# Attention with two-sided maxima: ScalarE presets the score banks, the row product goes, and the up projection moves ahead of the second maxima product

## The reference

```python
h = _layernorm(x, axis=-1) * (1 + ca) + sa
x = x + ga * _L0_attn_ref(h, ...)
h = _layernorm(x, axis=-1) * (1 + cb) + sb
x = x + gb * _L0_ffn_ref(h, ...)
```

## Time and profile before

| what | us |
|---|---|
| median of three runs | 906.31 |
| the profiled execution | 895.69 |
| its span | 893.96 |
| TensorE busy | 813.2 |
| VectorE busy | 637.1 |
| GpSimd busy | 662.7 |
| ScalarE busy | 397.2 |

### The profile page before, as it was taken

How to read it: one execution, slowest core, us unless ns; L and a number is a source line. 1 busy time by engine, 2 the same in 40 slices (tenths; PEclk the granted TensorE clock), 3 DMA queues, 4 the chain that set the end, 5 groups by cost and what they waited for, 6 DMA issues and landing times.

```text
span 894.0 us, 14690 instructions
## 1 busy us (share of the span) xinstructions
PE 813.2 (91%) x5118; PEld 485.9 (54%) x5118; DVE 637.1 (71%) x1156; ACT 397.2 (44%) x650; POOL 662.7 (74%) x348
## 2 busy tenths in 40 slices
PE   4689999999999999999999999999999977968581
PEld 2445555555555555555555555555555444368581
DVE  8987777777777777777777777777776757646022
ACT  3654444444444444444444444444444433336340
POOL 2579998898987878787878787878777856632333
PEclk8979999999999999999999999999999999969796
DMA  9101001010101011111011111101010000078683
GB/s 246 31 1 14 13 14 25 14 25 13 25 13 26 13 26 14 27 20 26 6 26 25 22 25 14 24 14 14 13 13 15 12 13 1 19 238 269 213 314 89
DMA packets 84330, 43.91 MB, mean 49 GB/s; under 512 B 57632, under 2 KB 73376, under 8 KB 84192
## 3 DMA queue, kind: packets, MB, share of 16 engines
q1 hardware_dynamic: 83232, 40.86, 18.2%
q0 software_dynamic: 1024, 2.10, 0.7%
HBM read 36.51 MB, written 6.16 MB: 48 GB/s over the span
## 4 chain that ended last, share of the span: by engine, by line
PE 82%; DVE 8%; DMA 4%; POOL 2%; issue 2%; ACT 1%; POOLq 0%; SPq 0%; DVEq 0%
PE ps_o L456 25%; PE ps_m L422 9%; PE ps_x L410 8%; PE ps_s L440 7%; PE ps_s L442 6%; PE ps_s L446 6%; PE ps_s L444 6%; PE ps_s L473 3%; DMA moe<-xs_dram 3%; PE ps_s L464 3%; PE ps_s L595 2%; PE ps_s L586 2%; POOL xs_dram L953 2%; DVE mx L1097 1%; PE ps_s L377 1%
## 5 line engine op out<-in xcount | busy, mean ns | idle before, releaser
L939 POOL TENSOR_TENSOR acc<-acc,probs 128x1024 f32<-128x1024 f32 (+1 forms) x192 | 459.9, 2395 | 74.7 <-ACT probs L697 52.5
L1097 DVE TENSOR_REDUCE mx<-ps_m 128x2 f32<-128x1024 f32 x240 | 293.7, 1224 | 90.9 <-PE ps_m L422 90.3
L697 ACT ACTIVATE probs<-ps_s 128x1024 f32<-128x1024 f32 x256 | 248.8, 1024 | 157.7 <-PE ps_s L446 157.6
L456 PE MATMUL ps_o<-probs,c_all 128*64 128x512 f32 x1024 | 249.5, 608 | 0.0
L440 PE MATMUL ps_s<-q_hi,k_hi 64*128 64x512 f32 x512 | 102.6, 397 | 12.0 <-DVE x_sb L1153 12.0
L456 PEld LDWEIGHTS ps_o<-probs,c_all 128*64 128x64 f32 x1024 | 62.4, 136 | 93.2 <-issue 44.5
L422 PE MATMUL ps_m<-k_hi,q_hi 64*128 64x512 f32 x480 | 107.7, 444 | 4.0 <-DVE mx L1097 4.0
L939 POOL TENSOR_TENSOR acc<-probs 128x1024 f32<-128x1024 f32 (+1 forms) x32 | 75.4, 2357 | 48.3 <-ACT probs L697 47.8
L442 PE MATMUL ps_s<-q_hi,k_lo 64*128 64x512 f32 x512 | 101.4, 391 | 0.0
L446 PE MATMUL ps_s<-neg_row,one_row 64*128 64x512 f32 x512 | 101.3, 391 | 0.0
L444 PE MATMUL ps_s<-q_lo,k_hi 64*128 64x512 f32 x512 | 100.8, 389 | 0.0
(11 more groups left out here) (299 smaller groups left out, 1025.5 us busy)
## 6 DMA issues: line engine op xcount, KB each, us to landing
probs<-in_experts SPq DMA_DIRECT2D x15, 578.0 KB, 6.0
rr<-rd_dram SPq DMA_DIRECT2D x62, 128.0 KB, 3.1
wu<-in_wqk SPq DMA_DIRECT2D x16, 256.0 KB, 3.4
neg_row<-nm SPq DMA_DIRECT2D x256, 0.5 KB, 2.0
w_first<-in_experts SPq DMA_DIRECT2D x5, 578.0 KB, 5.2
rot<-in_experts SPq DMA_DIRECT2D x5, 578.0 KB, 5.0
hT<-in_experts SPq DMA_DIRECT2D x5, 578.0 KB, 5.6
xs_dram<-zero SPq DMA_DIRECT2D x2, 960.0 KB, 9.4
```

Of the source, the lines that this page charges most:

```text
L456: ins = nc.tensor.matmul(ps_o[64 * h:64 * h + 64, :], c_all[:, (p // HP) * TB + kt, :], probs[:, st % 4, h, :], start=(kt == 0), stop=(kt ...
L697: nc.scalar.activation(probs[:, st % 4, :, :], ps_s[:, 2 * (st % 2):2 * (st % 2) + 2, :], ACT.Exp, scale=SCALE).then_inc(s["probs"], 1)
L939: V.tensor_tensor(acc[:, half, heads, :], first, probs[:, st % 4, heads, :], ALU.add).then_inc(s["added"], 1)
L1097: V.reduce_max(mx[:, :, kh, qt], max_banks(q, n), AX.X).then_inc(s["max_reduced"], 1)
```

## The change

ScalarE writes minus the maximum into a step's two score banks before TensorE adds the three remaining products to them (`start=False`). For that the maxima are spread over all partitions: each of the 8 columns of `nm` goes to a row in DRAM, and two DMAs spread it to `neg_wide`. The copy's halves for the banks 2 and 3 wait for the denominators' copy and for the output's addition, in ScalarE's order. On TensorE `up` stands ahead of the group's second maxima product, and the second value product of a group behind denominators and outputs. On VectorE the order in a group is reduce, turn, reduce, lower, and lower is that of the same group's unit. `upper` follows the exponentials and one preset of its own group.

```diff
@@ tensor: score
-                ge(pe, s["probs"], n_step(p, st) - 2)
-                if kt == 0:
-                    pe.wait_ge(row_placed[half], 128 * (p + 1))
-                if kt == 1:
-                    ge(pe, s["den_read"], n_part(p, half) - 2)
-                    ge(pe, s["out_added"], n_part(p, half) - 3)
+                pe.wait_ge(s["preset"], n_step(p, st))
...
-                    nc.tensor.matmul(bank[h], k_hi[rows(h), p % 3, kc], q_hi[rows(h), p % 3, qc], start=True, stop=False)
+                    nc.tensor.matmul(bank[h], k_hi[rows(h), p % 3, kc], q_hi[rows(h), p % 3, qc], start=False, stop=False, skip_group_check=True)
...
-                for h in range(2):
-                    ins = nc.tensor.matmul(bank[h], one_row[rows(h), :], neg_row[rows(h), p % 2, qc], start=False, stop=True)
@@ tensor: outputs
-                                           g_all[:, p // HP, p % HP, :], start=True, stop=True)
+                                           g_all[:, p // HP, p % HP, :], start=(n == 0), stop=(n == 3))
@@ tensor: a group
                     score(p, 2 * g)
                     score(p, 2 * g + 1)
+                    if p + 2 <= LAST:
+                        up(p + 2, g)
                     if p < LAST:
                         maxima(p + 1, 2 * g + 1)
...
-                    if p + 2 <= LAST:
-                        up(p + 2, g)
-                    for n in (2 * g - 2, 2 * g - 1):
+                    def value_step(n):
                         if n >= 0:
                             pv(p, n)
                         elif p > 0:
                             pv(p - 1, NSTEP + n)
+
+                    value_step(2 * g - 2)
                     if g in (3, 7):
                         pe.wait_ge(s["probs"], n_step(p, 2 * g + 1))
...
+                    value_step(2 * g - 1)
@@ scalar
+            def preset(p, st):
+
+                half, kt = divmod(st, TB)
+                if p == 0 and st < 2:
+                    act.wait_ge(s["max_reduced"], NMAX - 1 + st)
+                ge(act, s["probs"], n_step(p, st) - 2)
+                if kt == 0:
+                    act.wait_ge(row_wide[half], 32 * (p + 1))
+                if kt == 1 and (p or half):
+                    ge(act, s["den_read"], n_part(p, half) - 2)
+                    nc.scalar.copy(ps_s[:, 2, :], neg_wide[:, half, 0, :])
+                    ge(act, s["out_added"], n_part(p, half) - 3)
+                    nc.scalar.copy(ps_s[:, 3, :], neg_wide[:, half, 1, :]).then_inc(s["preset"], 1)
+                else:
+                    nc.scalar.copy(ps_s[:, 2 * (st % 2):2 * (st % 2) + 2, :], neg_wide[:, half, :, :]).then_inc(s["preset"], 1)
...
+            preset(0, 0)
+            preset(0, 1)
             for p in range(NPAIR):
                 for g in range(NGRP):
                     if g == 0 and p > 0:
                         den_out(p - 1, 0, ps_s[:, 2, :])
+                        preset(p, 1)
                     if g == 4 and p > 0:
                         den_out(p - 1, 1, ps_s[:, 2, :])
+                    if g == 4:
+                        preset(p, 9)
...
-                    if g == 0 and 2 <= p + 1 <= LAST:
-                        upper(p + 1, NGRP - 1)
-                    if g > 0 and p + 2 <= LAST:
-                        upper(p + 2, g - 1)
                     expo(p, 2 * g)
                     expo(p, 2 * g + 1)
+                    if g < NGRP - 1:
+                        preset(p, 2 * g + 2)
+                    elif p < LAST:
+                        preset(p + 1, 0)
+                    if p + 2 <= LAST:
+                        upper(p + 2, g)
+                    if g not in (3, NGRP - 1):
+                        preset(p, 2 * g + 3)
@@ vector
                     if p < LAST:
                         reduce_max(p + 1, 2 * g)
-                    q, u = (p + 2, g - 1) if g else (p + 1, NGRP - 1)
-                    if 2 <= q <= LAST:
-                        lower(q, u)
+                    if p + 2 <= LAST:
+                        turn(p + 2, g)
                     if p < LAST:
                         reduce_max(p + 1, 2 * g + 1)
                         if g % 4 == 3:
                             neg_max(p + 1, g // 4)
                     if p + 2 <= LAST:
-                        turn(p + 2, g)
+                        lower(p + 2, g)
@@ sync
                 for h in range(2):
                     for n in range(4):
-                        row = neg_row[64 * h:64 * h + 1, q % 2, half * HALF + n * P:half * HALF + (n + 1) * P]
-                        sp.dma_start(row.bitcast(F32), nm[:, half, h, n:n + 1].bitcast(F32)).then_inc(row_placed[half], 16)
+                        sp.dma_start(mr_dram[half, h:h + 1, n * P:(n + 1) * P], nm[:, half, h, n:n + 1]).then_inc(row_out[half], 16)
+
+            def max_spread(q, half):
+
+                sp.wait_ge(row_out[half], 128 * (q + 1))
+                if q:
+                    sp.wait_ge(s["preset"], n_step(q - 1, TB * half + TB - 1))
+                for h in range(2):
+                    sp.dma_start(neg_wide[:, half, h, :],
+                                 mr_dram[half, h:h + 1, :].to_broadcast([P, HALF])).then_inc(row_wide[half], 16)
...
                 if p > 0:
-                    if p < LAST + 1:
-                        max_rows(p, 1)
+                    max_rows(p, 1)
                     den_cols(p - 1, 0)
                     inv_rows(p - 1, 0)
+                    max_spread(p, 1)
                     inv_spread(p - 1, 0)
                 if p < LAST:
                     max_rows(p + 1, 0)
                 if p > 0:
                     den_cols(p - 1, 1)
                     inv_rows(p - 1, 1)
+                if p < LAST:
+                    max_spread(p + 1, 0)
+                if p > 0:
                     inv_spread(p - 1, 1)
```

More of the change, by code:

```diff
@@ L91, in build @@
         hi_of, lo_of = (q_hi, k_hi), (q_lo, k_lo)
-        one_row = sb("one_row", [P, P], F32R)
-        neg_row = sb("neg_row", [P, 2, S], F32R)
+        neg_wide = sb("neg_wide", [P, 2, 2, HALF])
         probs = sb("probs", [P, 4, 2, HALF])
@@ L96, in build @@
         mx = sb("mx", [P, 2, 2, TB])
-        nm = sb("nm", [P, 2, 2, 4], F32R)
+        nm = sb("nm", [P, 2, 2, 4])
         den = sb("den", [P, HALF])
@@ L107, in build @@
         rt_sb = sb("rt_sb", [P, 12, TB * E])
+        mr_dram = nc.dram_tensor("mr_dram", [2, 2, HALF], F32, kind="Internal").ap()
         rd_dram = nc.dram_tensor("rd_dram", [2, 2, HALF], F32, kind="Internal").ap()
@@ L211, in build @@
             "max_row": "both heads' maxima of half the queries, negated (vector)",
-            "scores": "both heads' scores of a step, less the maximum (tensor)",
+            "preset": "a step's score banks hold minus the maximum (scalar)",
+            "scores": "both heads' scores of a step, added to it (tensor)",
             "probs": "their probabilities (scalar)",
@@ L250, in build @@
         up_in = sem("up_in")
-        row_placed = [sem(f"row_placed{n}") for n in range(2)]
+        row_out = [sem(f"row_out{n}") for n in range(2)]
+        row_wide = [sem(f"row_wide{n}") for n in range(2)]
         den_cols_in, inv_out, inv_in = sem("den_cols_in"), sem("inv_out"), sem("inv_in")
@@ L439, in score @@
                 for h in range(2):
-                    nc.tensor.matmul(bank[h], k_hi[rows(h), p % 3, kc], q_hi[rows(h), p % 3, qc], start=True, stop=False)
+                    nc.tensor.matmul(bank[h], k_hi[rows(h), p % 3, kc], q_hi[rows(h), p % 3, qc], start=False, stop=False, skip_group_check=True)
                 for h in range(2):
-                    nc.tensor.matmul(bank[h], k_lo[rows(h), p % 3, kc], q_hi[rows(h), p % 3, qc], start=False, stop=False)
+                    nc.tensor.matmul(bank[h], k_lo[rows(h), p % 3, kc], q_hi[rows(h), p % 3, qc], start=False, stop=False, skip_group_check=True)
                 for h in range(2):
-                    nc.tensor.matmul(bank[h], k_hi[rows(h), p % 3, kc], q_lo[rows(h), p % 3, qc], start=False, stop=False)
-                for h in range(2):
-                    ins = nc.tensor.matmul(bank[h], one_row[rows(h), :], neg_row[rows(h), p % 2, qc], start=False, stop=True)
+                    ins = nc.tensor.matmul(bank[h], k_hi[rows(h), p % 3, kc], q_lo[rows(h), p % 3, qc], start=False, stop=True, skip_group_check=True)
                 ins.then_inc(s["scores"], 1)
@@ L1004, in then @@
                 dve.wait_ge(s["vector_step"], seq[0])
[L1006 to L1010, removed]
+            V.memset(ones[:], 1.0).then_inc(s["constants"], 1)
             def statistics(src, tiles):
@@ L1100, in neg_max @@
                 dve.wait_ge(s["max_reduced"], NMAX * q + TB * (half + 1))
-                ge(dve, row_placed[half], 128 * q)
+                ge(dve, row_out[half], 128 * q)
                 V.tensor_reduce(nm[:, half, :, :], mx[:, :, :, 4 * half:4 * half + 4].rearrange("p h k t -> p h t k"),
@@ L1378, in max_rows @@
```

(12 more changed lines are left out.)

## The result

The changed kernel takes 1078.31 us in the median of four runs (1068.44 to 1081.58), the kernel before, beside it, 903.71 (899.53 to 908.09): a ratio of 1.191, with an interval of 1.181 to 1.202. It is slower, as forecast, but by 175 us and not by 32. The time lies far outside the range of 892 to 955. Its profiled span is 1074.9.

What follows compares the result with a forecast made beforehand. The prediction took TensorE to bound the kernel before and a chain through VectorE the plain groups after. Halves of 3 x 5.07 + 8.22 = 23.43 against 22.07 gave +35, together with the ends +32: 938 us, range 892 to 955.

Steps and rivals of the forecast that it cites:

- The row DMAs keep their count and size: On SP's queue, the DMAs moving the maxima: said to stay the same in count and size, with no cost given.
- Four DMAs of broadcast per pair: The max_spread DMAs on SP's queue behind inv_rows: hidden, since SP waited some 2 us for inv_out there anyway.
- the start: At the kernel's beginning, two presets ahead of the first exponential: +1 us.
- Rival 3: Denominators' columns land late, so the reciprocal pushes turn by 0.5 us per half: +13, 951 us; chance 0.12.
- pair 14: Pair without up projection, so without the chain: its 8 groups could give 3.7 us back, 3 taken.
- The chain of the plain group: First maxima product, scores, up, turn, second reduction, next maxima product: 5.07 us a group, where it was 5.03.
- The division: In groups 2 and 6, VectorE's division catches GpSimd's addition 0.3 us after its start, running from 5.2 to 7.81.
- Rival 1: The division issues before GpSimd's addition and costs 0.68 us: total change -10.5, 896 us; chance 0.28.
- The closing group: Group 3 or 7, with denominators and output product: 6.56 plus 1.66 from the late division, 8.22 us instead of 6.98.
- Presets: ScalarE's 16 copies of 128x1024 into PSUM per pair: 1.02 us each, low end 0.92, hidden under the group.
- Rival 4: ScalarE becomes the bound, only from a preset of 1.45 us on; at 1.6, near 970 us; chance 0.04.
- Rival 2: TensorE stays the bound because a row of the chain overlaps: -47 us, with the ends 857; chance 0.04.

Runs made afterwards that it cites:

- e2: The changed kernel, with the row DMAs writing to SBUF as before and two 2 KB DMAs per half carrying the rows to DRAM: 950.17 us, ratio 1.058.
- e1: The changed kernel with SP's queue reordered, denominators' columns ahead of the row DMAs and inv_rows and inv_spread ahead of max_spread: 958.3 us, ratio 1.066.
- e3: The kernel before, with only its maxima rows sent through DRAM in 4-byte pieces and brought back by two 2 KB DMAs: 1034.92 us, ratio 1.153.
- e7: The kernel before plus eight DMAs of nm per half behind the columns, 4-byte pieces side by side in an unread DRAM buffer: 1053.78 us, one run.
- e8: e7 with the 4-byte pieces 256 bytes apart in DRAM: 901.08 us, one run.
- e4: The kernel before with only the new order on TensorE, VectorE and ScalarE, the row product kept: 970.94 us, ratio 1.079.
- e5: e2 with its presets but the kernel before's order on TensorE and VectorE, both presets ahead of upper: 885.63 us, ratio 0.986 to the kernel before.
- e9: e5 with one step of the values' product moved ahead of the second maxima product: 952.46 us, ratio 1.052 to the kernel before.
- e6: e2 with the division moved behind the closing group's first reduction: 909.03 us, ratio 1.011 to the kernel before.

## Why the prediction was wrong, point by point

**The step that failed** is the sentence "The row DMAs keep their count and size", with nothing costed behind it: a term of the sum put at nothing. Count and size are kept; the destination isn't. It went from SBUF to pieces side by side in DRAM. The profile before had no row of such a DMA (the nearest, of the reciprocals, has pieces of 16 bytes, and would have said 1.7 us). By the text's own manner its cost should have been bounded from both sides. What the runs show in its place: the columns behind these DMAs land late (after 9.26 us in the half shown), VectorE stands 3.9 us for them in the mean and 114.1 in all, and a half takes 28.3 instead of the forecast 23.4. The neighbouring "Four DMAs of broadcast per pair" were rightly called hidden behind the start: e2 has them too, and its division waits for `rr` only once, 5.1 us, as before. Rival 3 named the right wait (VectorE idle before rc) with the wrong cause and size: it took the landing at up to 3.6 us and the price at 0.5 per half. The sign it gave (VectorE idle before rc by over 1 us in most halves) did come.

How the span of 1074.9 stands to the 894.0 of before, by neg_max's intervals. Of the difference of 181, e2, without the failed step, makes 52.5:

| us | forecast | e2 | changed kernel |
|---|---|---|---|
| start, through the fourth interval | +3 | +6 | +16 |
| 25 inner halves | +34 | +43 | +155 |
| pair 14 and the end | -4 | +4 | +10 |

(Rounded. Inner halves: 22.09 before, 23.80 in e2, 28.30 in the changed kernel; 25 x 1.71 = 43, 25 x 6.21 = 155. The forecast had 25 x 1.36 = 34, and the 26th in the start.) The step that failed is the last column less the middle one, 128 us of span. Undone (e2, 1.058) or removed from the front of the queue (e1, 1.066), it goes or nearly so; put into the kernel before (e3, 1.153), it comes. What is left in e2 is 52.5 where the forecast had 32: the right mechanism, and 20 us too little.

The Trainium skill (DMA: Bandwidth & Descriptors, "Queues, rings and completion order") states that a DMA's semaphore increment is a strongly ordered write that lands only after every earlier write of that DMA engine, on any of its queues. Traces and runs agree with it: e1 moves the lateness to whatever is behind the rows (5.9 us for the reciprocals' DMA), and in e7 a DMA is late (6.5 us) that has nothing to do with the extra ones. That such writes should themselves take so long isn't in that rule. The same page ("Specifications") says that transfers below 512 bytes are done by read-modify-write. e8's pieces are as small, and are not late (1.6 us against 6.5), so that alone doesn't make it. That neighbours in one stretch of memory wait for each other would fit e7 and e8, but it was not measured by itself: the inner mechanism stays open.

**Right:**
- The chain of the plain group: predicted 5.07, measured 5.08 to 5.10 wherever the columns are in time, and 5.53 in e4 as it should be with the row product. TensorE's idle time there was to be about 0.5; it is 0.23 to 0.24, since its own work in this order is longer than the 4.57 of the text (below).
- The division: it catches the addition, predicted 2.61 (5.2 to 7.81), measured 2.61 (534.30) and 2.36 in the mean. Rival 1 (it escapes) fell, but it is right that phase decides: e5's order gives 0.81, e9's 2.41, e6's 1.09, with the same instruction.
- The closing group: predicted 8.22, measured 8.4. The text gave 0.04 for its changed order; the values in two blocks alone take 0.15 (e9).
- Presets: 1.02 predicted, 1.031 measured. Rival 4 fell. ScalarE waited 5.9 us for `neg_wide` in all, in the first preset.

Of the division, the text also says that no row shows one that issues ahead of the addition. The kernel before has one, in its last pair; VectorE's timeline, then GpSimd's:

```profile
739.84 0.68 DVE L1144 TENSOR_TENSOR ou<-ou,rr 128x512 f32<-128x512 f32 x1
```

```profile
739.98 2.80 POOL L939 TENSOR_TENSOR acc<-acc,probs 128x1024 f32<-128x1024 f32 x1
```

The division takes its 0.68, and the addition 2.80 instead of 2.37. So here the one that starts first is not delayed, and the other side of rival 1 could be read before the change too.

**Off in size, besides:** the start, +1 predicted. The first preset needs rows, then a spread, ahead of the first exponential. From ScalarE's timeline of the changed kernel:

```profile
66.79 1.96 ACT L712 COPY ps_s<-neg_wide 128x1024 f32<-128x1024 f32 x2 [5.87 <-DMA neg_wide<-mr_dram]
```

It took the place of a row that landed without anyone waiting: the first exponential starts at 70.07, in the kernel before at 66.82. In e2 the wait is 2.5, but the scores behind it run at a granted clock of 0.50 (61.8 to 68.5), where the kernel before has 1.00. And pair 14: -3 predicted, since it has no up projection, and +3 measured in e2 (22.9 and 23.5 against 21.1 and 22.3). Its plain groups fall only from 4.38 to 4.21, not by 0.46, and TensorE stands 2.31, 1.68 and 1.29 us in it (736.51, 754.24, 770.44) for VectorE's reductions and for a preset that waits for out_add; the kernel before stands 0.75, 1.04 and 1.06. The -3 rested on TensorE alone.

**TensorE's own work** was taken as 5.03 - 0.46 = 4.57 in every order, in the forecast, in rival 2 and in e5's expectation. It depends on the order, through the places where the shape changes (the distances of e9). In the changed kernel's order it is 5.09 - 0.24 = 4.85, in e9's 4.94 (worked out there). In e5's order 0.31 of the 4.88 come with the wait, and no run shows that order without it. In the kernel before, the row products covered the first reduction, so taking them away gives 0.15 per plain group and nothing in the closing ones. Rival 2's 857 would have needed both that order and something else for TensorE to do in the wait.

## What to carry to other kernels

A DMA's cost is also its destination: before you send something by way of DRAM in element-sized pieces, gather it in SBUF into a long row first, or put it behind everything in the queue that someone is waiting for. Count a landing by what is ahead of it in the queue, not by its own median. And an instruction that contends with GpSimd's is priced by its phase: look where it starts in each order that you try, since moving a TensorE product may move it (e9) and one place on VectorE may free it (e6).

## What the runs showed of the hardware that was not expected

- Eight DMAs of 128 pieces of 4 bytes, side by side in DRAM, put the wait for the next landing to 6.5 us in the mean (e7), and, in the changed kernel, a landing of the columns to 9.26 (3.9 us of waiting in the mean). The same pieces 256 bytes apart: 1.6 us (e8). The DMA engines show no work in the meantime (share 0.00 from 518 to 523).
- The length of a stall alone doesn't tell what TensorE's granted clock is behind it. In the changed kernel a closing group's stall of 1.42 us (538.20) is followed by 1.00, and one of 1.44 (446.95) by 0.50 (447.55 to 450.90): four value products take 1.88 us there and 1.08 elsewhere. In e9 the clock stays at 1.00 behind 23 of 26 stalls of about 1.7 us. After 5.30 us it was 0.50 at once. The two first, in the changed kernel:

```profile
538.20 0.49 PE L424 MATMUL ps_m<-k_hi,q_hi 64*128 64x512 f32 x2 [1.42 <-DVE mx L1116]
538.62 1.08 PE L451 MATMUL ps_o<-probs,c_all 128*64 128x512 f32 x4
```

```profile
446.95 0.50 PE L424 MATMUL ps_m<-k_hi,q_hi 64*128 64x512 f32 x2 [1.44 <-DVE mx L1116]
447.38 1.88 PE L451 MATMUL ps_o<-probs,c_all 128*64 128x512 f32 x4
```

- A copy of 1024 columns from SBUF into PSUM takes ScalarE 1.03 us, as an exponential out of PSUM does (1.02).
